# A two-layer recurrent kernel: from which step on pairs of input products are made by seven block products

## What is computed

```python
x = x + rnn(x, cond, L0_Wx, L0_Wh, L0_b)      # x: 32 x 128 x 512
x = x + lstm(x, cond, L1_Wx, L1_Wh, L1_b)
...
def step(prev_h, xw):                          # layer 0
    next_h = jnp.tanh(prev_h @ Wh + xw)        # xw = x_t @ Wx + b, Wx and Wh 512 x 512
...
def step(carry, xw_t):                         # layer 1
    prev_h, prev_c = carry
    a = xw_t + prev_h @ Wh                     # xw_t = x_t @ Wx + b, Wx and Wh 512 x 2048
    i, f, o = sigmoid of the first three quarters of a
    g = jnp.tanh(a[:, 3 * Hdim:])
    next_c = f * prev_c + i * g
    next_h = o * jnp.tanh(next_c)
```

## Time and profile before

| what | value |
|---|---|
| median of 3 runs | 851.63 us (851.48 to 855.56) |
| the profiled execution, its own time | 855.52 us |
| its span | 853.4 us |
| TensorE busy | 836.3 us, 98% |
| VectorE, ScalarE, GpSimd busy | 649.8, 578.2, 320.9 us |
| granted TensorE clock over the span | 0.999 |

### The profile page before, as it was taken

The page is one execution under the profiler, slowest core; times in us unless marked ns, Lnnn a source line. Parts: engine busy times, 40 slices in busy tenths (PEclk is TensorE's granted clock), DMA queues, the critical chain, the costliest instruction groups (busy, mean ns, idle before and its releaser), DMA issues.

```text
span 853.4 us, 51541 instructions
## 1 busy us (share of the span) xinstructions
PE 836.3 (98%) x22564; PEld 612.8 (72%) x22564; DVE 649.8 (76%) x1812; ACT 578.2 (68%) x1577; POOL 320.9 (38%) x677
## 2 busy tenths in 40 slices
PE   7999999999999999999999999999999999999996
PEld 4645665566677777777777777777777777777885
DVE  2668767776677878788787888778787887778765
ACT  2997466667667677676777767676776767777642
POOL 0312244445243433434343443434344343444320
PEclk9999999999999999999999999999999999999999
DMA  8801001111011111001111000111100000000000
GB/s 276 305 19 27 16 16 27 28 28 26 6 28 28 29 28 29 17 17 28 29 29 29 23 23 17 28 29 29 29 23 23 17 16 17 17 17 17 16 13 19
DMA packets 40193, 30.67 MB, mean 36 GB/s; under 512 B 5772, under 2 KB 38688, under 8 KB 38688
## 3 DMA queue, kind: packets, MB, share of 16 engines
q1 hardware_dynamic: 39712, 27.27, 11.1%
q10 hardware_dynamic: 256, 0.11, 0.0%
HBM read 18.95 MB, written 8.39 MB: 32 GB/s over the span
## 4 chain that ended last, share of the span: by engine, by line
PE 94%; DVE 2%; ACT 2%; DMA 1%; issue 1%; SPq 0%; ACTq 0%; DVEq 0%
PE ps_l L1265 36%; PE ps_l L1331 26%; PE ps_r L1406 9%; PE ps_r L1426 9%; PE ps_l L1309 7%; PE ps_l L1278 2%; PE ps_l L1298 2%; PE ps_r L1388 1%; PE ps_r L1377 1%; DMA whr_raw<-in_L_cond_Wh 1%; DVE pre_l L1069 0%; ACT whl_lo L703 0%; PE ps_l L1450 0%; PE ps_l L1252 0%; PE ps_l L1242 0%
## 5 line engine op out<-in xcount | busy, mean ns | idle before, releaser
L492 POOL TENSOR_TENSOR xb<-xb,h_l 128x128 f32<-128x128 f32 x127 | 58.0, 457 | 417.0 <-DVE h_lo L1115 413.5
L1265 PE MATMUL ps_l<-whl_hi,hT_hi 128*32 128x512 f16 x1888 | 122.7, 379 | 1.1 <-DVE hT_hi L1099 1.1
L1265 PE MATMUL ps_l<-whl_lo,hT_hi 128*32 128x512 f16 x1888 | 122.7, 379 | 0.0
L1265 PE MATMUL ps_l<-whl_hi,hT_lo 128*32 128x512 f16 x1888 | 122.7, 379 | 0.0
L1331 PE MATMUL ps_l<-whl_raw,wxl_raw 128*32 128x256 f16 x3600 | 115.8, 273 | 1.7 <-ACT wxl_raw L691 1.3
L1331 PE MATMUL ps_l<-wxl_hi,wxl_raw 128*32 128x256 f16 x2400 | 114.7, 273 | 0.0
L1331 PEld LDWEIGHTS ps_l<-whl_raw,wxl_raw 128*32 128x32 f16 x3600 | 96.3, 97 | 15.1 <-ACT ps_l L672 2.7
L786 ACT ACTIVATE gates<-pre_l 128x256 f32<-128x256 f32 x100 | 41.8, 418 | 93.5 <-DVE pre_l L1069 93.5
L1265 PEld LDWEIGHTS ps_l<-whl_lo,hT_hi 128*32 128x32 f16 x1888 | 51.2, 97 | 50.8
L1265 PEld LDWEIGHTS ps_l<-whl_hi,hT_lo 128*32 128x32 f16 x1888 | 51.2, 97 | 50.8
L1069 DVE SCALAR_TENSOR_TENSOR pre_l<-ps_l,g_products,wxl_raw 128x256 f32<-128x256 f32 x100 | 44.0, 480 | 44.3 <-PE ps_l L1265 39.6
(11 more groups left out here) (173 smaller groups left out, 1945.2 us busy)
## 6 DMA issues: line engine op xcount, KB each, us to landing
xb<-in_x SPq DMA_DIRECT2D x128, 64.0 KB, 2.2
out<-xb SPq DMA_DIRECT2D x124, 64.0 KB, 1.8
whl_raw<-in_L_cond_Wh SPq DMA_DIRECT2D x4, 1024.0 KB, 9.3
wxl_raw<-in_L_cond_Wx SPq DMA_DIRECT2D x4, 1024.0 KB, 8.0
wxr_raw<-in_L_cond_Wx SPq DMA_DIRECT2D x1, 1024.0 KB, 7.7
whr_raw<-in_L_cond_Wh SPq DMA_DIRECT2D x1, 1024.0 KB, 9.6
out<-xb SPq DMA_DIRECT2D x4, 48.0 KB, 2.0
wxl_raw<-peaks SPq DMA_DIRECT2D x5, 2.0 KB, 1.9
```

The lines of the kernel that those rows point to most:

```text
L492: nc.gpsimd.tensor_tensor(xb[g % NX][:, t, :], xb[g % NX][:, t, :], h_l[s % 2][:, :], ALU.add).then_inc(out_done, 1)
L1265: last = nc.tensor.matmul(ps_l[s % 4][quarter(j), :], (hT_hi, hT_lo)[h_part][:, k, :], gate_slice(whl[w_part][k], j), start=False, stop=(h ...
```

## The change

`S2` goes from 28 to 20. So steps 20 to 27 are made as four pairs, and `G2`, which ends the groups of y for single products, goes from 7 to 5. The blocks T1 to T4 have to be there earlier: three pieces a tick from tick 13 on instead of two from tick 15, and their eight halves of splits in ticks 15, 17, 18, 19, 21, 22, 23 and 25. The constants come in tick 22. TensorE waits for six of the eight splits ahead of the first pair's second part, and for all eight only ahead of M4.

```diff
-S2 = 28
+S2 = 20
...
-        T_MADE_AT = {15 + i: range(2 * i, 2 * i + 2) for i in range(16)}
-        T_HIGH_AT = {17 + 2 * i: [(T_ORDER[i // 2], i % 2)] for i in range(8)}
-        T_LOW_AT = {17 + 2 * i: [(T_ORDER[i // 2], i % 2)] for i in range(8)}
-        CONST_AT = 30
+        T_MADE_AT = {13 + i: range(3 * i, min(32, 3 * i + 3)) for i in range(11)}
+        T_HIGH_AT = {k: [(T_ORDER[i // 2], i % 2)] for i, k in enumerate((15, 17, 18, 19, 21, 22, 23, 25))}
+        T_LOW_AT = T_HIGH_AT
+        CONST_AT = 22
...
             def pair_second(p):
                 if p == 0:
-                    pe.wait_ge(t_split, 8)
+                    pe.wait_ge(t_split, 6)
...
                 block_product(p, 2, ALL[3:])
+                if p == 0:
+                    pe.wait_ge(t_split, 8)
                 block_product(p, 4, ALL, pair_mm)
```

## The result

The changed kernel takes **858.75 us** (median of 4 runs, 858.22 to 860.38), the kernel before 851.59 (4 runs, 851.48 to 855.56): a ratio of 1.0078, 95% interval 1.0060 to 1.0095. It is slower by over 0.5%, and above the range of 850.4 to 855.8. The profiled execution took 858.56 us with a span of 856.8.

What follows compares the result with a forecast made beforehand. TensorE was taken to bound the kernel. From 851.6 us: stalls 3.79, less 0.17 old stall and 2.36 gain, give +1.3; with third-piece meetings +2.2, so 853.8 us, range 850.4 to 855.8.

Steps and rivals of the forecast that it cites:

- Slower: Rival: GpSimd and VectorE meet more often, also at x low halves and the cell; 5.3 us slower, 856.9 us; chance 0.09.
- What bounds the kernel: TensorE, 94% of the chain; other engines cost nothing while their results come before TensorE asks for them.
- The gain of 2.36 us: Four more pairs, steps 20 to 27, each save TensorE 0.59 us against single products: 2.36 us in all.
- the old stall: TensorE's 0.17 us wait at a first-layer block of 24 in tick 32, which the change would remove.
- The stacked halves, 3.79 us: Block halves beside other extra work on ScalarE and VectorE make gates late; TensorE stalls behind ticks 18 to 25: 3.79 us.
- The free lateness of the gates, 3.75 us: Gates may start up to 3.75 us into a tick free; each us behind that is a us of the whole.
- The third piece: GpSimd's third piece per tick meets VectorE's low halves in ticks 17, 18, 21, 22: 0 to 1.8 us, 0.9 taken.
- One meeting of two, at 0.45: Piece and low half start within 0.1 us, so one meeting of two was taken each time, 0.45 us each.
- No tick there runs late.: Reason for taking 0 for pieces meeting VectorE's first-layer weight splits in ticks 13 and 14; bounds 0 and 0.45 us.
- The condition of the rival: The 0.09 rival decides from about 1.2 us of GpSimd and VectorE meetings beyond the forecast's upper end of +3.1 us.
- The waits for the splits of the blocks: TensorE's new wait for block 4's split in tick 26 costs 0, with only 0.5 us of cover.
- The lengths of ticks: Sign in the profile after: TensorE's ticks 24 to 33 should be 6.2 us long where nothing waits.

## Why the prediction was wrong

The forecast was 853.8 us, 2.2 above the kernel before, in the range 850.4 to 855.8; it came out 6.2 us above in the traces and 7.2 by the medians. What happened is the rival *Slower*, which had 5.3 us and a chance of 0.09.

- **What bounds the kernel:** right. All gaps are the first layer's block of 24 waiting for hT_r_hi and hT_r_lo.
- **The gain of 2.36 us, and 0.17 for the old stall:** right; 205.75 measured where the sum gives 205.70.
- **The stacked halves, 3.79 us:** right in sum, 3.74 by the gaps without pieces, less 0.20 given back in tick 27. By tick it was 0.80 (I had 0.88), none (0.20), 1.14 (0.88), 1.02 (1.03) and 0.78 (0.80): tick 20 hid what I charged it with, and tick 23 was later than a repeat of tick 19.
- **The free lateness of the gates, 3.75 us:** right. Counted from TensorE's own starts, which lie 0.17 ahead of the chain's, it is 3.92, and the gaps of the change follow from it, with what the cell took over 1.40: tick 19 has gates at 5.65, so 1.73 (measured 1.72); tick 16 has 4.54 and a cell 0.43 slower, so 1.05 (1.04); tick 23 has 5.99 and 0.46, so 2.53 (2.53).
- **The third piece: the step that failed.** I took 0.9 us, with an upper end of 1.8; the runs show 5.1. It was mis-sized in three ways. (1) *One meeting of two, at 0.45.* Every one of the four took place, and they cost 0.45, 0.57, 0.47 and 0.44: the upper end, not the middle. "If VectorE comes first each time it is 0" was wrong too: in tick 18 the low half started 0.03 ahead of the piece and had the dearest meeting. (2) *Only block halves in the crowded ticks were counted.* The splits of tick 13 (0.95), the low half of tick 15 (0.2), the y low half of tick 16 (2.20 from pre_r to the turn instead of 1.99), the cells of ticks 15, 16 and 23 (0.35 to 0.46 each) and the input's low half of tick 22 (0.4, from GpSimd's bias and y blocks, which I had set at 0 as "some 3 us before ScalarE asks for the blocks": I asked who waits for them, not whom they meet) were left out. (3) *"No tick there runs late."* True of ticks 13 to 15, and no reason: the gates of tick 16 came 1.3 us later than without pieces, though no tick up to it had waited. That made the gap of tick 16. I also started tick 18 from the old 3.55, and the trace starts it from 4.65: 0.45 of this is the meeting of tick 17, and the rest comes from the low half of tick 15 and from the y low half and the cell of tick 16, since with the first six pieces cut it is still 4.61. The runs with the last 26 and with the first six cut show the part of the six: 0.7 us by themselves, 1.1 together with the rest. The other 4 us are the meetings of ticks 15 to 22 and what is passed on.
- **The condition of the rival:** it named these things (the x low half, the cell's small products, lateness passed on), and stood against "small products between pieces show 0.29 in most ticks". That was read from ticks with two pieces, where GpSimd is done before the cell. With three it is not. In the halves that it had at full price it also came short, as it had the same start of tick 18.
- **The waits for the splits of the blocks:** right, no gap. **The lengths of ticks:** ticks 28 to 33 are 6.2 us, as said, but the ones from 24 on are those of the first pair (7.15, 8.78, 6.19 and 6.82 without waits), as the sum itself had it. **The level:** the median of three runs was at the low end of the scatter; later comparisons have the kernel before 2 to 3 us higher. This takes about 1 us off the miss, not the rest.

What stays open: what the 0.20 and 0.14 us are that a meeting costs less than what is left of the other instruction, what sets the start of tick 9, and the gap of tick 43 in one run.
